# One block for expert combine, Mamba preparation and scan, with the preparation in halves of four batches

## What is computed

```python
# experts: each token's four rows, weighted
y = jnp.sum(outs * topk_weight[..., None], axis=1)
x = x + y
# Mamba block, on layernorm(x); residual is layernorm(x) too
xn = x * jax.lax.rsqrt(jnp.mean(x * x, axis=-1, keepdims=True) + EPS) * norm_w
x_inner, z = jnp.split(jnp.einsum('bld,ed->ble', xn, in_proj_w), 2, axis=-1)   # 512 + 512
xc = _silu(conv4(x_inner, conv_w) + conv_b)            # 4 taps along time, per channel
x_ssm = jnp.einsum('bld,ed->ble', xc, x_proj_w)        # 16 B, 16 C, 1 dt
dt = jax.nn.softplus(x_ssm[..., -1:] * dt_w[:, 0] + dt_b)
A = -jnp.exp(A_log)                                    # 512 channels x 16 states
def step(h, inp):                                      # along time
    dt_t, B_t, C_t, u_t = inp
    h = jnp.exp(dt_t[..., None] * A) * h + (dt_t * u_t)[..., None] * B_t[:, None, :]
    return h, jnp.sum(h * C_t[:, None, :], axis=-1) + D_param * u_t
return jnp.einsum('ble,de->bld', y * _silu(z), out_proj_w) + residual
```

## Time and profile before

| | us |
|---|---|
| median of 3 executions | 972.68 |
| the profiled execution | 972.43 |
| its span | 970.7 |
| busy in the span: PE, DVE, ACT, POOL | 766.6, 746.2, 523.5, 517.4 |
| combine block: first to last instruction | 553.5 to 600.6 |
| preparation block | 601.1 to 664.2 |
| scan: first scan instruction | 666.9 |

### The profile page before, as it was taken

One profiled execution on the slowest core, in us unless ns is written; L12 is line 12 of the kernel. 1 busy time (PEld: TensorE's weight loads), 2 busy tenths in 40 slices (PEclk: granted clock), 3 DMA queues, 4 the chain that ended last, 5 costly groups with the idle time before them and its releaser, 6 DMA issues. The chain is left out here.

```text
span 970.7 us, 14534 instructions
## 1 busy us (share of the span) xinstructions
PE 766.6 (79%) x4329; PEld 549.3 (57%) x4329; DVE 746.2 (77%) x1507; ACT 523.5 (54%) x1341; POOL 517.4 (53%) x535
## 2 busy tenths in 40 slices
PE   6798999999999988059999605885999999960255
PEld 2467888888888775047777402334555555540133
DVE  1585777888888965867777556987899999779977
ACT  0223555556556645026666402588888788309085
POOL 1002777777777864635555273303798788623210
PEclk9779999999999989569999857896999999995576
DMA  8805300000000300015555454003223222010000
GB/s 273 288 0 216 132 1 2 1 7 7 2 7 6 154 33 12 6 43 147 144 147 140 124 158 142 1 3 109 76 98 109 87 95 101 22 44 0 1 13 32
DMA packets 30188, 72.45 MB, mean 75 GB/s; under 512 B 5648, under 2 KB 19728, under 8 KB 27616
## 3 DMA queue, kind: packets, MB, share of 16 engines
q1 hardware_dynamic: 25504, 58.93, 17.5%
q0 software_dynamic: 4608, 12.59, 5.2%
HBM read 60.96 MB, written 10.55 MB: 74 GB/s over the span
## 5 line engine op out<-in xcount | busy, mean ns | idle before, releaser
L1739 POOL TENSOR_TENSOR arena<-arena 128x1024 f32<-128x1024 f32 x63 | 147.5, 2368 | 30.9 <-DVE arena L1705 30.9
L1705 DVE TENSOR_TENSOR_SCAN arena<-arena,ps 128x1024 f32<-128x1024 f32 x64 | 143.5, 2276 | 14.1 <-PE ps L1626 8.2
L1646 PE MATMUL ps<-arena 128*128 128x512 f32 x256 | 120.1, 592 | 0.0
L782 ACT ACTIVATE arena<-arena 128x128 f32<-128x128 f32 x256 | 98.8, 390 | 11.3 <-DVE arena L723 11.3
L608 PE MATMUL ps<-arena 128*128 128x128 f32 (+1 forms) x768 | 100.7, 281 | 0.8 <-PEq L345 0.8
L823 POOL TENSOR_TENSOR arena<-arena 128x256 f32<-128x256 f32 x64 | 47.6, 744 | 97.7 <-DVE arena L709 97.6
L608 PEld LDWEIGHTS ps<-arena 128*128 128x128 f32 (+1 forms) x768 | 91.6, 193 | 13.5 <-issue 11.9
L1036 POOL DMA_INDIRECT arena<-tokens,arena x64 | 61.9, 968 | 68.2 <-PE ps L1057 49.8
L790 ACT ACTIVATE arena<-ps 128x512 f32<-128x512 f32 x64 | 38.2, 597 | 88.1 <-PE ps L627 88.1
L1671 ACT ACTIVATE arena<-arena 128x1016 f32<-128x1016 f32 x64 | 72.5, 1135 | 22.8 <-DVE arena L1705 22.8
L1681 ACT ACTIVATE arena<-arena 128x256 f32<-128x256 f32 x192 | 81.3, 494 | 0.0
(11 more groups left out here) (319 smaller groups left out, 1674.7 us busy)
## 6 DMA issues: line engine op xcount, KB each, us to landing
arena<-c_rows SPq DMA_DIRECT2D x32, 512.0 KB, 3.6
arena<-in_E_gu SPq DMA_DIRECT2D x8, 1024.0 KB, 12.0
expert_out<-arena SPq DMA_DIRECT2D x64, 128.0 KB
arena<-in_E_dn SPq DMA_DIRECT2D x1, 4096.0 KB, 13.0
arena<-in_ctxT SPq DMA_DIRECT2D x2, 1024.0 KB, 4.9
arena<-in_X_o SPq DMA_DIRECT2D x1, 2048.0 KB, 20.6
arena<-in_A_o SPq DMA_DIRECT2D x1, 2048.0 KB, 27.5
arena<-in_F_w SPq DMA_DIRECT2D x2, 1024.0 KB
```

Source lines behind the costliest of these rows:

```text
L782: t = eng.activation(pr[:, i % 3, j, :], sm[:, d, j, :], ACT.Exp, bias=negm[:, d, j:j + 1], scale=SCALE[slots[i][0]], accum_out=rsum[:, i ...
L1646: t = eng.matmul(ps[:, 2 * k + half, :], ident, hC[s % 4][:, half * 512:(half + 1) * 512], start=False, stop=n == ST - 1)
L1705: eng.tensor_tensor_scan(hst[s % 4], dA[s % 4], psD[s % 2].rearrange("p k m -> p (k m)"), 0.0, ALU.mult, ALU.add).then_inc(h_ready, 1)
L1739: eng.tensor_tensor(hC[s % 4], hst[s % 4], Csb[i % 4], ALU.mult).then_inc(hC_ready, 1)
```

## The change

The three blocks become one. In it:

- SyncE issues all loads of `w1`, `w2`, `M_vec`, `M_in`, `M_bc` and `M_out` (3.8 MB together) at the start of the experts' block, ahead of the first store, as soon as VectorE has made `spread`.
- The gathers go through a ring of four batches. GpSimd waits for `combined` before it reuses a place; each of the four gathers of a batch has a semaphore of its own. Eight small memsets stand behind the first four gathers.
- ScalarE sums the magnitudes first. VectorE rounds `w1` ahead of combining batch 0, and `w2` ahead of batch 1.
- Products, convolution, Silu, B/C/dt product, softplus' Abs and Exp, and the split run in halves `k` of 512 tokens. Convolution of the first half stands between the combining of batches 4 to 7. VectorE convolves all four groups; ScalarE's and GpSimd's share is gone.
- B, C and dt come from one product of 97 columns; a product of one row with ones spreads dt over the partitions. Abs is taken from PSUM.
- The residual in `x` is made by GpSimd. ScalarE makes `diagD`.
- `dtu` of groups 0 and 1 is made ahead of slot 0, that of groups 2 and 3 after slot 1; the turns and copies of all four stand inside the scan's loops. The gate's second half is copied raw and gets its Silu after state 8, inside the scan.

```diff
             @block.sync
             def _(eng):
+                eng.wait_ge(spread_step, 2)
+                load(eng, "w1", w1, a["F_w1"])
+                load(eng, "w2", w2, a["F_w2"])
+                load(eng, "vecs", vecs, a["M_vec"])
+                load(eng, "w_in", w_in, a["M_in"])
+                load(eng, "w_bc", w_bc, a["M_bc"])
+                load(eng, "w_out", w_out, a["M_out"])
                 for s in range(NBLK):
...
             @block.tensor
             def _(eng):
+                def project(m, bank, k):
+                    for c in range(DC):
+                        t = eng.matmul(ps[:, bank, :], w_in[:, c, m * P:(m + 1) * P], half(hT[:, c], k),
+                                       start=c == 0, stop=c == DC - 1)
+                    return t
+                def bc_dt(k):
+                    for c in range(CT):
+                        eng.wait_ge(xc_ready, CT * k + c + 1)
+                        t = eng.matmul(ps[0:3 * E + 1, PROJ_BANK[k], :], w_bc[:, c, :], half(xc[:, c], k),
+                                       start=c == 0, stop=c == CT - 1)
+                    t.then_inc(proj_done, 1)
+                def dt_rows(k):
+                    eng.wait_ge(bcf_ready, k + 1)
+                    eng.matmul(ps[:, k, :], ones[3 * E:3 * E + 1, :], half(bcf[3 * E:3 * E + 1], k),
+                               start=True, stop=True).then_inc(dt_done, 1)
...
+                for m in range(CT):
+                    project(m, XI_BANK[1][m], 1).then_inc(xi_done, 1)
+                bc_dt(0)
+                project(CT, Z_BANK[1][0], 1).then_inc(z_done, 1)
+                dt_rows(0)
+                eng.wait_ge(xi_ready, 2 * CT)
+                bc_dt(1)
+                dt_rows(1)
+                for m in range(1, CT):
+                    project(CT + m, Z_BANK[1][m], 1).then_inc(z_done, 1)
...
             @block.scalar
             def _(eng):
+                for n in range(CT):
+                    xi(n, 1)
+                bc_rows(0)
+                magnitudes(0)
+                for n in range(CT):
+                    conv_silu(n, 1)
+                bc_rows(1)
+                exponentials(0)
+                eng.activation(negA, negA, ACT.Exp).then_inc(s_negA, 1)
+                magnitudes(1)
+                exponentials(1)
+                for m in (0, 1):
+                    eng.wait_ge(z_done, CT + m + 1)
+                    eng.activation(half(zs[:, m], 1), ps[:, Z_BANK[1][m], :], ACT.Copy).then_inc(z_moved, 1)
+                eng.wait_ge(exp_ready, 2 * CT)
+                for c in range(CT):
+                    eng.activation(dtu[:, c], dtu[:, c], ACT.Ln, bias=1.0).then_inc(ln_dt, 1)
...
                 for i in range(2 * ST):
                     scaled(i, 0, NB // 2)
                     decay(2 * i)
+                    if i == 0:
+                        turned_dtu(0)
                     scaled(i, NB // 2, NB)
                     decay(2 * i + 1)
+                    if i == 0:
+                        turned_dtu(1)
+                    if i == 1:
+                        turned_dtu(2)
+                        turned_dtu(3)
+                    if i == ST // 2:
+                        eng.wait_ge(z_moved, 2)
+                        eng.wait_ge(z_moved_v, 2)
+                        eng.activation(zs[:, :, HT:], zs[:, :, HT:], ACT.Silu).then_inc(zs_ready, 1)
...
             @block.vector
             def _(eng):
+                ternary(eng, cw_, 0, w1, w1q)
+                combine(0)
+                ternary(eng, cw_, 1, w2, w2q)
+                for b in range(1, HB):
+                    combine(b)
+                normS.dve_variance(eng, 0)
+                scales_in(eng, cs, 0)
+                scales_out(eng, cs, 0)
+                combine(HB)
+                for c in range(CT - 1):
+                    conv(c, 0)
+                    combine(HB + 1 + c)
+                normS.dve_variance(eng, 1)
+                scales_in(eng, cs, 1)
+                scales_out(eng, cs, 1)
+                conv(CT - 1, 0)
+                for c in range(CT):
+                    conv(c, 1)
+                steps(0)
+                split(0)
...
+                split(1)
+                steps(1)
...
+                dt_and_dtu(0)
+                dt_and_dtu(1)
...
                 for s in range(SLOTS):
                     if direct(s):
                         dBu_of(s)
                     scan(s)
+                    if s == 1:
+                        dt_and_dtu(2)
+                        dt_and_dtu(3)
...
             @block.gpsimd
             def _(eng):
+                for b in range(NB):
+                    if b >= 4:
+                        eng.wait_ge(combined, b - 3)
+                    for k in range(TOPK):
...
+                for b in range(NB):
+                    eng.tensor_scalar(x[:, b, :], x[:, b, :], rstd[:, b:b + 1], mean_rstd[:, b:b + 1], ALU.mult,
+                                      ALU.subtract)
```

520 lines of the change are left out of this document (234 added, 286 removed).

## The result

The changed kernel takes 978.52 us, median of 9 runs (974.31 to 979.16), beside 971.71 for the kernel before (9 runs, 966.74 to 976.13): the ratio is 1.0073, 95% interval 1.0052 to 1.0093. It is slower by 0.7%, clear of the noise; 965.6 us and "faster" were forecast, and the time lies above the range of 956 to 975. Its profiled execution took 974.31 us, with a span of 972.6.

The account below looks back on a forecast made before the run. Experts and scan were taken as bound by work, combining and preparation by waits. Against 972.43, -17.0 + 6.0 + 1.0 + 2.0 + 1.0 = -7.0 gave 965.4, forecast as 965.6 us; 8-in-10 range 956 to 975.

Parts of the forecast that it names:

- Slot 0 scans at 649.9, 17.0 us earlier: End of preparation: the first scan was to start at 649.9 instead of 666.91, 17.0 us saved.
- the replay: Combining and preparation: each changed instruction placed by engine order and waits on the profiled clock, from block start 553.5.
- Gathers land by 597, so they no longer decide: First half's convolutions between batches 4 to 7: VectorE, not the gathers, was to set the pace, until 606.6.
- Gathers beside rounding: Start of combining: six wide VectorE instructions beside GpSimd's gathers were to cost +1.0 us, bounds 0 and 7.5.
- Gathers blocked by rounding: Rival, start of combining: no descriptors during wide roundings, batches 1 to 3 7.5 us late, 972 in all; chance 0.08.
- I take 1.0: Preparation, B/C/dt product of half 1: 1.0 us allowed for TensorE slowed after idling 3 us.
- start of the scan: Slots 0 to 6: turns, copies and two `dtu` now inside the scan were to cost +6.0 us, bounds 0 and 10.
- Silu in the scan: Inside the scan: the gate's Silu and two table loads on ScalarE were to cost +1.0 us, bounds 0 and 4.5.
- loads in the experts' stage: Experts' stage: 3.8 MB of early loads delaying stores and gathers were to cost +2.0 us, bounds 0 and 14.
- GpSimd's residual beside convolutions: Second half's convolutions: GpSimd's eight residual instructions beside them were to add 1.4 us.
- Loads stop the experts: Rival, experts' stage: early gathers and first four stores wait behind 3.8 MB, up to 14 us, 977.6; chance 0.12.

Follow-up runs that it names:

- g2: Changed kernel without late gathers, roundings moved behind VectorE's convolutions, one z product put ahead of the second B, C, dt product: 962.87 us, one run.
- f2: Changed kernel with the 16 gathers of batches 4 to 7 left out (second half of the output not the reference's): 964.30 us, one run.
- f1: Changed kernel unchanged, timed on another chip as the mark for its group: 976.72 us, ratio 1.0068 to the kernel before.
- h1: Changed kernel unchanged, timed on a chip that showed no late completions: 969.70 us, ratio 1.0020 to the kernel before.
- i1: Changed kernel unchanged, one look on a further chip: 968.92 us, one run.
- f3: Changed kernel with one z product of the second half moved ahead of the second B, C, dt product: 974.29 us, ratio 1.0036 to the kernel before.
- h2: Changed kernel with the late gathers bringing a quarter of each row: 968.24 us, ratio 1.0014 to the kernel before.
- i2: Changed kernel with the late gathers bringing a quarter of each row, on a further chip: 963.64 us, one run.
- e1: Changed kernel unchanged, one more look: 972.94 us, one run.
- e4: Changed kernel with ScalarE's root for the second half moved ahead of three convolution Silus: 974.18 us, ratio 1.0011 to the kernel before.
- g1: Changed kernel with the 16 gathers of batches 4 to 7 bringing a quarter of each row: 966.58 us, one run.
- h3: The kernel before, unchanged, run for its own profile on a chip without late completions: 968.30 us, one run.
- f4: Changed kernel reordered: roundings on ScalarE, most convolutions behind the combines, root and turns earlier, z products ahead of B, C, dt: 961.39 us, ratio 0.9891 to before.
- e2: Changed kernel with both weight roundings moved from between the first gathers to behind convolutions: 973.57 us, ratio 1.0009 to the kernel before.

## Why the prediction was wrong

The step that failed is "Slot 0 scans at 649.9, 17.0 us earlier". Measured were 3.0. g2 puts slot 0 at +95.2 where the step had +95, and its stations before that lie within 0.7 us of the replay's: `h` at 580.3 and 605.9 for 580.7 and 606.6, the last convolution at 625.4 for 626.0. So the dependences and durations of the replay were right. That the last station fits to 0.2 us is partly luck, since g2 pays nothing of the 1.0 us allowed for TensorE's idle time and has its roundings elsewhere on VectorE. Three things lay on top, 13.9 us in all, 8.6 from f2 and 5.3 from g2 against f2.

- *Completions told late, 8.6 us (f2 against the first profile of the changed kernel; 8.9 against f1; h1 and i1, with their gathers but without the delay, are 7.9 and 8.7 sooner).* "Gathers land by 597, so they no longer decide" took a gather as something that others wait for only when they need its data. On chips with the delay the semaphores of TensorE and VectorE rise late beside them too, and in f2, without them, they don't. The kernel before lost 1.4 us; nothing of what it computes there but its combines is waited for soon (one product ended at 593.08 and was told at 598.61, and delayed nobody). The changed kernel puts a chain of product, copy and convolution there. No rival had this. The trace of before showed it, and I passed over it: VectorE's linked combines waited 0.91 and 1.14 us for themselves.

```profile
594.99 0.48 DVE L1328 SCALAR_TENSOR_TENSOR arena<-arena 128x256 f32<-128x256 f32 x1 [0.91 <-DVE arena L1328]
597.80 0.48 DVE L1328 SCALAR_TENSOR_TENSOR arena<-arena 128x256 f32<-128x256 f32 x1 [1.14 <-DVE arena L1328]
```

- *Gathers beside rounding, 4.0 us (g2 against f2), for "+1.0" and 0.5 for the memsets.* The rival "Gathers blocked by rounding" had the mechanism and 7.5 us; beside six roundings three gathers paid, up to 1.37 us, about a whole rounding instruction (1.32). The rule in the Trainium skill ("SBUF — State Buffer", the box on the "DVE blocks DMA" trap) is borne out here as to the wide instructions, and the row of 0.99 that I priced it by had narrow ones. A range from 0 to 7.5 was right; the choice of its lower end was not.
- *TensorE's idle time, "I take 1.0", 1.3 more (g2, what is left of the 5.3), 3.2 in all in f3 against f1.* The row that I used had 5.32 us for eight records after 3.72 us of idle time. After 3.48 or 3.49 us the changed product takes 5.01 to 5.19 us in five profiles (f2, h1, h2, i1, i2), as that row says, and 6.28 to 6.61 in seven (the first, e1 to e4, f1, g1), by how much of it runs at the lower clock: 0.70 granted on average in h1, 0.55 in the first. The mechanism was right, the price too small for the second kind. Late completions don't make the difference, since g1 has none and takes 6.46; what does stays open.

The rest, by its terms: start of the scan +6.0, measured 6.5; Silu in the scan +1.0, measured 0.3; loads in the experts' stage +2.0, measured 1.5 (in the other profiles with these loads -0.1 to 2.3); GpSimd's residual beside convolutions 1.4, measured 0.9 (steps of 2.51 to 2.65 for 2.33). "Loads stop the experts" is out. Measured, the terms are -3.0, which has the gathers' term in it, 6.5, 0.3 and 1.5: +5.3, and 0.8 behind slot 63 makes +6.1. The medians differ by 6.8, with 5.1 to 9.0 as the interval.

Without the delay the forecast would have failed too: in h1 and i1 slot 0 is at +101.2 and +100.4, still 5 to 6 us short of the step, and h1's time is not below that of the kernel before (1.0020; i1's single run is 2.8 us below it).

What stays open: h1's profile is 3.5 us shorter than h3's, and its ten timed runs are 2.0 us longer than before (-0.2 to 4.2). Every profile is of one execution, and h1's was the fastest of its ten (964.82, median 969.70), so most of these five lie between executions of one kernel; the parts ahead of the change alone vary by up to 6.7 us. In which stage they lie isn't known. How much of the loss in time is the delay's is open as well: with the delay the ratio was 1.0073 and 1.0068 but near 1 in e1's single run, without it 1.0020. And "chip" may stand for something else, since each chip served on one occasion only.

That the recording of the trace itself makes the delay, when the records of the landings overflow, is possible: each execution timed here was recorded, and no run tells. The Trainium skill ("NOTIFIC — the notification-queue block", 7.1 Overflow: three behaviours, one of which stalls the engine) states that the block which writes such records can hold up the engines when an internal queue is full; this case shows lost records and late completions together, not which causes which.

## What to carry to other kernels

A stage that waits for many small gathers isn't free room: a chain of short dependent steps put beside them can pay at each hand-over (0.9 to 2.3 us for VectorE's linked steps in f4), and wide VectorE instructions stretch the issue of gathers (by up to 1.37 us each here). Put there what has few hand-overs and runs on another engine (here the roundings on ScalarE, in 23 us that it sat idle). And when a trace shows an instruction that waits a microsecond for the one before it on its own engine, ask what delays completions before adding dependent work at that place.

## What was not expected of the hardware

- Completions told late beside gathers, in the first measurement and on two chips of five: TensorE's up to 8.5 us in e1 and 10.6 in f4 (a product ended at 589.38 and was told at 600.01), VectorE's in f4 in steps of 1.40 us (584.58, 585.99, 587.38, 588.78, 590.18). On the other three chips they were told within 0.02 us (h1).
- GpSimd's four memsets of 128x24 took 1.20 us beside a rounding and 0.30 without (e2).
- The same product of 97 columns took 6.53 us at a mean granted clock of 0.55, 5.19 at 0.70 (both after 3.5 us of idle time) and 3.67 at 1.00 (f3, after 1.48 us).
- ScalarE rounds a 128x2048 weight in four passes of 2 us and hardly stretches a gather: in f4 fifteen of the first sixteen take 0.94 or 0.95 us, one 1.16.
